# Keys and values of four heads moved from the third layer's gate into the first layer, and one stash store moved behind the row of state 9

## The reference, cut to what matters

```python
def _L0_xattn_ref(hidden_states, z, in_proj_w, conv_w, conv_b, x_proj_w, dt_proj_w, dt_proj_b, A_log, D):
    x = jnp.einsum('bld,ed->bel', hidden_states, in_proj_w)
    ...
    def step(state, inp):
        d, b, c, u = inp
        dA = jnp.exp(d[..., None] * A)
        state = state * dA + (d * u)[..., None] * b[:, None, :]
        y = jnp.einsum('bdn,bn->bd', state, c)
        return (state, y)
    ...
    y = y + D[None, :, None] * x
    y = y * silu(z)

def _L3_xattn_ref(hidden_states, encoder_hidden_states, Wq, Wk, Wv, Wo, gq, gk):
    ...
    k = (encoder_hidden_states @ Wk).reshape(B, Skv, H, D)
    v = (encoder_hidden_states @ Wv).reshape(B, Skv, H, D)
    ...

x = x + jnp.tanh(g_xattn[0]) * _L0_xattn_ref(ctx_1024, _layernorm(x, axis=-1), ...)
x = x + jnp.tanh(g_ffn[0]) * _L0_ffn_ref(_layernorm(x, axis=-1), ...)
...
x = x + jnp.tanh(g_xattn[2]) * _L2_xattn_ref(ctx_1024, _layernorm(x, axis=-1), ...)
x = x + jnp.tanh(g_ffn[2]) * _L2_ffn_ref(_layernorm(x, axis=-1), ...)
x = x + jnp.tanh(g_xattn[3]) * _L3_xattn_ref(_layernorm(x, axis=-1), ctx_1024, ...)
```

## Time and profile before

| | |
|---|---|
| median of 3 runs | 3713.45 us (3708.44 to 3716.21) |
| the profiled execution | 3708.7 us, of which the span is 3707.1 us |
| PE busy | 3437.8 us (93%) |
| DVE busy | 3013.5 us (81%) |
| ACT busy | 1759.9 us (47%) |
| POOL busy | 623.9 us (17%) |
| mean granted TensorE clock | 0.966 of 2.4 GHz |

### The profile page before, as it was taken

How to read it: one execution, slowest core, us unless ns; L and a number is a source line. 1 busy time by engine, 2 the same in 40 slices (tenths; PEclk the granted TensorE clock), 3 DMA queues, 4 the chain that set the end, 5 groups by cost and what they waited for, 6 DMA issues and landing times.

```text
span 3707.1 us, 40267 instructions
## 1 busy us (share of the span) xinstructions
PE 3437.8 (93%) x12305; PEld 1947.9 (53%) x12322; DVE 3013.5 (81%) x4951; ACT 1759.9 (47%) x2748; POOL 623.9 (17%) x596
## 2 busy tenths in 40 slices
PE   7888888799999999899999899999999999999887
PEld 4667676544444444444445788655455455455443
DVE  8899998797979798789889867688388388388797
ACT  6878787633333223334443311255155155155297
POOL 2324251243433220134331000000000000000000
PEclk9899988999999999999999999999999999999998
DMA  4324241524342322443444300221021022021000
GB/s 156 133 65 148 66 147 59 196 86 147 102 153 93 137 84 92 156 153 97 149 156 175 145 24 23 104 70 60 31 70 60 21 70 70 20 70 64 32 12 34
DMA packets 91260, 345.73 MB, mean 93 GB/s; under 512 B 11841, under 2 KB 20161, under 8 KB 77793
## 3 DMA queue, kind: packets, MB, share of 16 engines
q1 hardware_dynamic: 61552, 226.90, 17.4%
q0 software_dynamic: 29552, 116.94, 9.6%
HBM read 280.88 MB, written 62.91 MB: 93 GB/s over the span
## 4 chain that ended last, share of the span: by engine, by line
PE 48%; DVE 27%; issue 14%; ACT 6%; DMA 3%; DVEq 0%; POOL 0%; ACTq 0%; POOLq 0%; SPq 0%
PE ps L1213 30%; PE ps L1610 6%; PE ps L1600 3%; DVE room L1782 3%; PE ps L1441 2%; DVE room L1786 2%; DMA room<-bc_scratch 2%; DVE room L1790 2%; PE ps L1493 2%; PE ps L1282 2%; DVE room L1852 1%; DVE room L1795 1%; DVE room L1850 1%; ACT room L871 1%; DVE room L2320 1%
## 5 line engine op out<-in xcount | busy, mean ns | idle before, releaser
L1213 PE MATMUL ps<-lnT,room 128*128 128x512 f32 x2240 | 987.0, 596 | 23.1 <-DVE room L2007 16.0
L1213 PEld LDWEIGHTS ps<-lnT,room 128*128 128x128 f32 x2240 | 426.0, 191 | 567.9 <-issue 525.5
L1213 PE MATMUL ps<-room 128*128 128x512 f32 (+2 forms) x1807 | 666.8, 524 | 49.6 <-ACT room L1138 21.1
L680 POOL TENSOR_TENSOR idle<-idle 128x1 f32<-128x1 f32 x268 | 447.1, 1668 | 1263.4 <-ACT room L881 434.6
L1213 PEld LDWEIGHTS ps<-room 128*128 128x128 f32 (+1 forms) x1824 | 289.9, 163 | 404.5 <-issue 258.4
L1441 PE MATMUL ps<-room 128*128 128x512 f32 x864 | 379.7, 597 | 8.5 <-DVE room L1961 8.5
L792 ACT ACTIVATE room<-room,small 128x511 f32<-128x511 f32 x256 | 163.6, 710 | 380.6 <-DVE room L1786 380.5
L1852 DVE TENSOR_TENSOR_SCAN room<-room 128x2048 f32<-128x2048 f32 x64 | 283.2, 4425 | 19.0 <-ACT room L871 13.8
L1786 DVE TENSOR_TENSOR_SCAN room<-room 128x2048 f32<-128x2048 f32 x64 | 283.4, 4428 | 5.9 <-DVE room L1782 0.9
L1441 PEld LDWEIGHTS ps<-room 128*128 128x128 f32 x864 | 165.1, 192 | 215.2 <-issue 208.3
L1112 ACT ACTIVATE room<-ps,stat 128x512 f32<-128x512 f32 x256 | 199.0, 777 | 137.3 <-DVE stat L2268 137.3
(11 more groups left out here) (284 smaller groups left out, 5105.1 us busy)
## 6 DMA issues: line engine op xcount, KB each, us to landing
room<-in_ffn SPq DMA_DIRECT2D x16, 2048.0 KB, 10.9
room<-bc_scratch POOLq DMA_DIRECT2D x128, 256.0 KB, 3.6
room<-kv_stash SPq DMA_DIRECT2D x64, 512.0 KB, 3.4
kv_stash<-room POOLq DMA_DIRECT2D x96, 256.0 KB, 2.4
room<-stash POOLq DMA_DIRECT2D x24, 1024.0 KB, 5.2
room<-in_ffn SPq DMA_DIRECT2D x20, 1024.0 KB, 5.1
room<-in_ffn SPq DMA_DIRECT2D x24, 768.0 KB, 5.6
room<-in_ffn SPq DMA_DIRECT2D x12, 1536.0 KB, 7.3
```

The lines of the kernel that those rows point to most:

```text
L680: nc.gpsimd.tensor_tensor(idle[:, :], idle[:, :], idle[:, :], ALU.add).then_inc(zeros_added, 1)
L1213: last = nc.tensor.matmul(out, lhsT, rhs, start=(i == 0), stop=(i == len(parts) - 1))
```

## The change

All sixteen heads of a batch are made in stage 0, four more units per batch. The table has 16 entries: units at n = 1, 3, 14, 14 and 15 are new, and n = 8 has one unit where it had two. Twelve of them (n = 1 to 12) are the batch's own, four (n = 13, 14, 14, 15) the next batch's. The context load for these four moves from n = 10 to n = 13 in SP's program. The store of `m_z` moves from n = 8 to n = 9 there. `gate_mamba` loses the 16 units, their context and weight loads, their copies and their stores, and each wait on them. The waits of `ffn8` and `attention3` on those stores go too.

```diff
-KV_HEADS, KV_LEAD = 12, 4
-KV_OWN = KV_HEADS - KV_LEAD
-KV_ORDER = (4, 5, 6, 6, 7, 8, 8, 9, 10, 11, 12, 13)
+H, KV_LEAD = 16, 4
+KV_OWN = H - KV_LEAD
+KV_ORDER = (1, 3, 4, 5, 6, 6, 7, 8, 9, 10, 11, 12, 13, 14, 14, 15)
...
-                        if n == 10 and not last:
+                        if n == 13 and not last:
                             sp.wait_ge(tile_filled, tile("kv", KV_OWN - 1, 1)[0] + 1)
                             sp.dma_start(m_kctx, ctx_d[bass.ds(b * P + P, P), :]).then_inc(kctx_loaded, 16)
...
-                        if n == 8:
+                        if n == 9:
                             place = stashed(2, b)
                             sp.wait_ge(Du_ready, b + 1)
                             sp.dma_start(place, m_z).then_inc(Du_stored, 16)
...
             def gate_mamba(stage):
-                sp.wait_ge(a_qk, 2 * B)
-                sp.dma_start(ctx[:, :], ctx_d[0:P, :]).then_inc(gk_loaded[0], 16)
                 sp.wait_ge(s_y_added, 2 * B * STATES)
-                for i in range(LATE):
-                    h = KV_HEADS + i
-                    sp.dma_start(g_kvw[:, i * HEAD_KV:(i + 1) * HEAD_KV], head_d[h * P:(h + 1) * P, HEAD_Q:]
-                                 ).then_inc(gkw_loaded, 16)
                 sp.wait_ge(x_done, B * stage)
...
-                units(0, 1)
                 gate(0)
-                units(1, 2)
                 gate(1)
-                units(2, 5)
                 gate(2)
-                widen(0, 2)
-                units(5, 9)
-                widen(2, 4)
+                widen(0, 4)
                 gate(3)
                 widen(4, 6)
-                units(9, 13)
                 take_lnT(stage + 1, 0)
                 widen(6, EARLY)
-                units(13, B * LATE)
...
-                pe.wait_ge(gkw_loaded, LATE * 16)
-                units(0, 3)
                 gate(0)
-                units(3, 6)
                 gate(1)
-                units(6, 10)
                 gate(2)
-                units(10, 13)
-                pe.wait_ge(gk_taken, 26)
                 transpose_ln(stage + 1, 0)
                 gate(3)
                 pe.wait_ge(lnT_ready, B * LNT[stage + 1] + 1)
-                units(13, B * LATE)
```

More of the change, by code:

```diff
@@ L95 @@
 SLOT = 4 * TILE_COLS
-H, HD = 16, 128
+HD = 128
 HEAD_Q, HEAD_KV = NK * HD, CK * 2 * HD
@@ L755, in _ @@
                 feed_states(3, 1)
-                for k in range(B * LATE):
-                    store_late(k)
             if stages > 1:
                 pool.wait_ge(s_y_stored, B * 16 * (2 if stages > 3 else 1))
-            if stages > 3:
-                for i in range(3):
-                    pool.wait_ge(gk_stored[i], GK_STORES[i] * 16)
             if stages > 6:
@@ L923, in body @@
                         if late is not None:
-                            take_kv(late, b * (KV_HEADS * 16) + (KV_LEAD + late) * 16, tile)
+                            take_kv(late, b * (H * 16) + (KV_LEAD + late) * 16, tile)
                         if n == 6:
@@ L980, in gate @@
                     nc.scalar.activation(g_z[b % 2], ln[:, :], ACT.Silu).then_inc(g_z_ready, 1)
-                def units(first, last):
-                    for k in range(first, last):
-                        if k >= 3:
-                            act.wait_ge(gk_stored[k % 3], k // 3 * 16)
-                        for half in range(2):
-                            act.wait_ge(gk_filled, 2 * k + half + 1)
-                            nc.scalar.activation(g_kv[k % 3][:, half * 4 * HD:(half + 1) * 4 * HD],
-                                                 ps[:, 4 + 2 * (k % 2) + half, :], ACT.Copy).then_inc(gk_taken, 1)
                 def widen(first, last):
@@ L1358, in gate_mamba @@
             def gate_mamba(stage):
-                w4 = g_kvw.rearrange("p (i c n) -> p i c n", i=LATE, c=CK)
-                def units(first, last):
-                    for k in range(first, last):
-                        b, i = divmod(k, LATE)
-                        if i == 0:
-                            pe.wait_ge(gk_loaded[b % 2], b // 2 * 16 + 16)
-                        if k >= 2:
-                            pe.wait_ge(gk_taken, 2 * k - 2)
-                        for half in range(2):
-                            for j in range(2):
-                                t = 2 * half + j
-                                mm = product(ps[:, 4 + 2 * (k % 2) + half, j * 256:(j + 1) * 256],
-                                             [(g_kctx[b % 2][:, c, t * P:(t + 1) * P], w4[:, i, c, :]) for c in range(CK)])
-                            mm.then_inc(gk_filled, 1)
                 def gate(b):
@@ L2066, in body @@
                             t = g * n + j
-                            if first and t == n:
-                                for i in range(3):
-                                    dve.wait_ge(gk_stored[i], GK_STORES[i] * 16)
                             dve.wait_ge(up_done, b * T + (base + t + 1))
```

39 lines of the change are left out of this document (10 added, 29 removed).

## The result

The changed kernel takes 3745.05 us (median of 4 runs, 3740.65 to 3750.16), the kernel before 3712.81 us (3708.44 to 3716.21, 4 runs) on the same chip. The ratio is 1.0088, 95% interval 1.0070 to 1.0105: 32 us slower. I had said 3733 us, with 3708 to 3752 as the range, and slower as the likeliest sign.

What follows compares the result with a forecast made beforehand. DVE was taken to set stage 0's pace, with PE nearly as busy. The terms, -18.7 + 5.8 + 28.2 + 9 - 1.5 = +22.8 us on 3708.7 us (median 3713.45), gave 3733 us, range 3708 to 3752.

Steps and rivals of the forecast that it cites:

- Row 9 and the unit of n = 8: Stage 0: DVE's waits for row 9 go and `exp_abs` comes sooner; 3 x -4.7 - 4.6 = -18.7 us.
- the cap that I drew from ACT's chain: Stage 0, n = 8: ACT's chain comes about 4.7 us sooner, capping the gain per batch in batches 0 to 2.
- Early units: Stage 0, units at n = 1 and 3: ahead of transposes for ACT's decays; 3.7 + 3 x 0.7 = +5.8 us.
- the 3 us that should come back from a faster PE: Head of batches 1 to 3: shorter PE idle gives a faster clock, 3 us back in each.
- Context load and row 14: Stage 0, state 14: row 14 late behind PE's fill, load and store; 9.9 x 2 + 8.4 = +28.2 us.
- the three late units: Stage 0, units at n = 14, 14 and 15: ACT's copies wait for stores; 3 x 3 = +9 us.
- The last batch: Stage 0: no context load, so row 9's gain less the early units; -4.6 + 0.7 = -3.9 us.
- The gate: Stage 4: without units waits shrink and `ffn8` starts sooner (-9.5 us), PE's lower clock takes most back; net -1.5 us.
- B: Rival: PE keeps full clock from state 11, row 14 lands quickly, both effects cancel; 3708 to 3714 us, chance 0.14.
- C: Rival: row 14 is in time, DVE keeps row 9's 18.7 us, so faster; 3687 us, chance 0.12.
- D: Rival: PE becomes the bound of stage 0, all 16 units showing in full; 3750 us and more, chance 0.12.

Runs made afterwards that it cites:

- twelve_moved: stash_move_alone with the second unit of n = 8 moved to the end and the context load from n = 10 to n = 11: 3687.39 us, 0.9937.
- twelve_stash_later: twelve_moved with the two 1 MB stash stores of states 11 and 13 one state later each: 3685.8 us, 0.9944.
- store_behind_row14: The changed kernel with the 1 MB store of state 13 behind row 14, the context load staying ahead of it: 3733.66 us, 1.0069.
- row14_first: The changed kernel with the context load, and its wait on PE, behind row 14 in SP's program: 3737.39 us, 1.0078.
- single_late_units: The changed kernel with one unit instead of two at n = 14 and a new unit at n = 0: 3719.59 us, 1.0022.
- row14_first_hold: row14_first with SP waiting for the last stores of keys and values before it loads for the next stage: 3735.06 us, 1.0062.
- gate_warm: The changed kernel with unused transposes of the identity filling PE's idle stretches in the third layer's gate: 3743.43 us, 1.0100.
- load_at_12: single_late_units with a unit at n = 2, none at n = 11, and the context load at n = 12: 3720.78 us, 1.0025.
- stash_move_alone: The kernel before with only the store of `m_z` moved behind the row of state 9, twelve heads as before: 3697.85 us, 0.9968.

## Why the prediction was right in its sign and too low in its size

**Row 9 and the unit of n = 8** (-18.7 us predicted). Right in kind, too small: DVE doesn't wait for row 9 nor, more than 0.34 us, for `exp_abs` in batches 1 to 3, so 6.9, 6.1 and 6.3 us went where I gave 4.7; the last batch won 4.6 + 1.4. The step that failed is the cap that I drew from ACT's chain: I took it to come 4.7 us sooner without the second unit of n = 8. twelve_moved, which has no early unit that could hold DVE back, waits there 0.36, 0.95 and 0 us, so the chain came 4.69 + 1.75 - 0.95 = 5.5 us sooner (second batch). Over the four batches this term came to -25.2 us.

**Early units** (+5.8). The first half was right: I gave 3.7 us a batch and 3.45 was measured in the first three, 2.5 in the last. The step that failed is the 3 us that should come back from a faster PE at the head of batches 1 to 3. PE's idle ahead of the transposes did shrink to 2 or 3 us as I said, but in two of the three heads the transposes stayed slow: 5.35 and 6.63 us, where they had taken 6.62 and 6.64. In the head between them they were quick, and PE then stood still:

```profile
418.14 3.71 PE L1234 MATMUL ps<-ident,room 128*128 128x128 f32 x32 [2.08 <-DVE room L1823]
424.84 3.69 PE L1264 MATMUL ps<-room 128*128 128x512 f32 x8 [2.98 <-issue]
```

Before, 32 transposes took 6.59 us from 393.24 and the next product followed at 399.66, 6.42 us after their start; now it follows 6.70 us after. In the head ahead of this one it follows 8.48 us after (6.46 before), behind a stop of 3.13 us, and in the last batch's 6.47 (6.48). So none of the 3 x 3 = 9 us came back. It was not a fixed delay that the slow transposes had hidden: in twelve_stash_later the transposes take 3.71 us and the product follows 3.55 us after their start in all three heads, with no stop. What differs is in the DMA views. Two of the three heads lie behind the jump of PE's loop, 28 such heads in the fourteen traces. In the 22 with a stop (1.97 to 3.60 us, put down to "issue"), and in one where the view names ACT for the gap, the queue that the profile calls "instruction" moves one to three packets of 16 KB at the head; in the five without any stop, both of the kernel before among them, it moves none. That PE waited for its own program there is the likely reading; no run tests it.

**Context load and row 14** (+28.2). PE's fill, the order of SP's issues and DVE's need came within 1.1 us of the count. The step that failed is the landing: I took 6.7 us, and row 14 took 10.4. The three waits are 11.04, 13.07 and 12.40 us, 36.5 in all: +8.3 on this term. The figure was misread. It is the middle of two rows, of which only one stood between the load and the store; the other stood behind both, as row 14 does now. The DMA view of the kernel before has the first alone from 508.3 to 509 us and the second alone from 509.5 to 512 us:

```profile
room<-bc_scratch SPq DMA_DIRECT2D x1, 256.0 KB, 4.3
```

```profile
room<-bc_scratch SPq DMA_DIRECT2D x1, 256.0 KB, 9.2
```

With 9.2 us in place of 6.7 my own sum gives 12.4 us for the third batch, 10.9 for the first and 35.7 in all, beside the 36.5 measured. By the rule of the Trainium skill's page DMA: Bandwidth & Descriptors (Anatomy of one DMA) the row would have landed 5.0 us after its issue; the trace says 10.4. Without the store ahead the same rule gives, as an estimate, 3.2 us, and the trace of store_behind_row14 says 5.5. That section is on DMAs issued by GpSimd, while these are SP's, and its formula has no term for what else the 16 engines carry.

What a wait is worth is another matter. I had added row 14 and **the three late units** (+9, of which 2.10 + 2.15 + 2.40 = 6.7 us appeared) as if each were a cost of its own. row14_first shows that, with row 14 in time, DVE waits 36.2 us at y all the same, where 8.5 us stood before. Some 7 to 11 us go with the store (store_behind_row14), and no more if the row is in time altogether; another 17 to 21 us, by the ratios, go only when the late units are thinned out too (single_late_units against these two). I argued that "the wait for row 14 covers the unit of n = 13"; it covered most of the work of all four units, and they covered most of it. The two terms added up only because each was seen with the other in place.

**The last batch** (-3.9). It was +6.0, an error of 9.9 us and the largest in the sum. I had only taken away its row 9, and had not asked what stands next to the units that now reach up to n = 12: the loads of the next stage. row14_first_hold shows it: with these loads held back the wait of 5.90 us goes.

**The gate** (-1.5; -2.4 measured). The clock took back most of what the units gave, as said: transposes of 3.34 us instead of 1.97, waits of 1.2 to 1.4 us at three gates and 2.42 at the last, `ffn8` late. gate_warm shows the mechanism in the trace, 6.6 us; its median doesn't prove it.

**The total.** It stayed inside the range partly by luck. Row 9 and the unit of n = 8 gave 6.5 us more than I had put down, which hid part of the 9 us of the early units, the 8.3 us of row 14 and the 9.9 us of the last batch.

**Rivals.** B and C needed row 14 in time. row14_first had it in time and was not faster than the changed kernel by anything that shows in its ratio, so C's rule, that row 14 decides, was wrong even as a condition. D, PE as the bound, is the nearest to what remains: with both late causes away, load_at_12 is 33 us above twelve_moved. The gate gives 2 us back, so the sixteen new units, 58 us of PE at 3.6 us each, cost 35 us in stage 0: some 0.6 of each unit's time shows, most of it at the head of the batch, where DVE waits for PE's transposes and projections. D had every unit show in full, 38 us above the kernel before. load_at_12 stands 9 us above it; that the changed kernel stands 32 above is in good part row 14 and the late units, so its nearness to 38 doesn't bear D out.

What stays open: which of ACT, POOL and PE sets the pace of the four late units in row14_first, since POOL's tiny additions, ACT's waits for stores and PE's for weights all grow there; whether the stop behind PE's loop jump is its program being fetched, and why it comes in some kernels and not in others; and why most of stash_move_alone's gain in the trace lies behind stage 0.

## What to carry to other kernels

Two waits that end near each other are not two terms: before a wait is priced, ask what would be waited for if it were gone, by following the other engines from the same starting event (here PE's fill of n = 12) to the next place where the engines meet. A median over two transfers is not the time of either: look at each alone, and take the one that stands as yours will. Place can matter more than amount: two units cost 12 us more at states 1 and 3 than at 9 and 10, and a small transfer landed 5 us later with a 1 MB store issued ahead of it than with the store behind it. When a stage's work reaches further towards its end, look at the prefetches of the next stage that start there.

## What the runs showed of the hardware that was not expected

- Behind the jump of PE's loop over batches PE stood still for 1.97 to 3.60 us in 22 of 28 cases with no releaser in the profile. In each of these, and in none of the five without a gap, the "instruction" queue moved packets of 16 KB. In the changed kernel's third batch the stop of 2.98 us took back what quick transposes (3.71 us instead of 6.59) had gained.
- Transposes of the identity, kept up with PE busy 61.4 of 64 us, went with a granted clock of 1.00 through the gate (0.61 without them), and 16 real transposes between them took 1.97 us instead of 3.34.
- An addition of one element per partition on POOL takes from 0.18 us to 4.34 us in the changed kernel's first 800 us. In the changed kernel's third batch there are:

```profile
554.96 3.71 POOL L660 TENSOR_TENSOR idle<-idle 128x1 f32<-128x1 f32 x1
...
561.85 0.18 POOL L660 TENSOR_TENSOR idle<-idle 128x1 f32<-128x1 f32 x1 [0.44 <-ACT room L850]
```

  The short one falls into DVE's wait for row 14, the long one into its work. POOL issues its stores behind these additions, so a busy DVE makes stores late; that DVE's wait at row 14 covered some of this too is argued, not shown. The Trainium skill's page SBUF — State Buffer (SBUF: two separate sides) says that DVE operations with two inputs in that memory and GpSimd's shut each other out for a whole instruction; the trace agrees: the addition of 3.71 us began inside a scan of DVE's (554.26 to 558.68 us) and ended with it, at 558.67, and the one of 0.18 us had none beside it.
